# Reordering the four score rounds of an attention segment: keys in the first round, value products in the other three

## The reference

```
x = x + attention0(layernorm(x), ctx)      # 16 heads of 64, softmax over 1024 context rows
x = x + experts0(layernorm(x))             # 32 experts, 6 of them per token, and 2 shared chunks
x = x + attention1(layernorm(x), ctx)
x = x + experts1(layernorm(x))             # 8 experts, one per token, and a shared one

def attention(x, c):                       # x: 4 x 512 x 256, c: 4 x 1024 x 192
    q, k, v = x @ Wq, c @ Wk, c @ Wv       # split in 16 heads
    p = softmax(q @ k.T / 8)
    return (p @ v) @ Wo + bo
```

## Time and profile before

| what | value |
|---|---|
| median of 3 runs | 2790.21 us |
| profiled execution, its own time | 2784.74 us |
| profiled execution, its span | 2783.1 us |
| mean granted TensorE clock | 0.967 |
| TensorE matmul busy | 2576.6 us (93%) |
| VectorE busy | 2074.2 us (75%) |
| GpSimd busy | 1513.9 us (54%) |
| ScalarE busy | 1283.3 us (46%) |

### The profile page before, as it was taken

The page is one execution under the profiler, slowest core; times in us unless marked ns, Lnnn a source line. Parts: engine busy times, 40 slices in busy tenths (PEclk is TensorE's granted clock), DMA queues, the critical chain, the costliest instruction groups (busy, mean ns, idle before and its releaser), DMA issues. The chain is left out here.

```text
span 2783.1 us, 37259 instructions
## 1 busy us (share of the span) xinstructions
PE 2576.6 (93%) x13254; PEld 1779.0 (64%) x13254; DVE 2074.2 (75%) x2464; ACT 1283.3 (46%) x1776; POOL 1513.9 (54%) x1132
## 2 busy tenths in 40 slices
PE   4999999999999689999999689999999999996895
PEld 3656565656565378888888555656565656554784
DVE  5677777777877577777777667777777777765795
ACT  3545454545554333333333345545454545443384
POOL 2777777777786511111111158777777777671345
PEclk8999999999999799999999789999999999997998
DMA  3211221221211100000000021112112121104212
GB/s 108 55 52 43 61 52 52 57 56 42 67 42 48 48 31 27 23 23 23 23 28 17 17 77 49 51 54 55 52 54 59 42 55 42 48 21 161 83 50 88
DMA packets 60160, 141.65 MB, mean 51 GB/s; under 512 B 8448, under 2 KB 21632, under 8 KB 59008
## 3 DMA queue, kind: packets, MB, share of 16 engines
q1 hardware_dynamic: 55184, 132.73, 16.6%
q0 software_dynamic: 1536, 4.20, 0.5%
q10 hardware_dynamic: 3312, 3.02, 0.3%
HBM read 79.36 MB, written 10.22 MB: 32 GB/s over the span
## 5 line engine op out<-in xcount | busy, mean ns | idle before, releaser
L382 POOL TENSOR_TENSOR L0a_psums<-L0a_psums,L0a_probs 128x512 f32<-128x512 f32 x384 | 488.1, 1302 | 21.5 <-ACT L0a_probs L439 17.3
L382 POOL TENSOR_TENSOR L1a_psums<-L1a_psums,L1a_probs 128x512 f32<-128x512 f32 x384 | 488.1, 1301 | 21.5 <-ACT L1a_probs L439 17.3
L516 DVE TENSOR_REDUCE L0a_row_max<-psum 128x2 f32<-128x2048 f32 x128 | 293.6, 2294 | 77.1 <-PE psum L653 76.1
L516 DVE TENSOR_REDUCE L1a_row_max<-psum 128x2 f32<-128x2048 f32 x128 | 293.6, 2294 | 76.8 <-PE psum L653 75.8
L876 POOL TENSOR_TENSOR L0e_w_lo<-L0e_raw,L0e_w_hi 128x768 fp32r<-128x768 f32 x34 | 63.8, 1876 | 496.9 <-ACT L0e_w_hi L890 496.9
L439 ACT ACTIVATE L1a_probs<-psum 128x1024 f32<-128x1024 f32 x256 | 253.2, 1026 | 116.7 <-PE psum L677 116.6
L439 ACT ACTIVATE L0a_probs<-psum 128x1024 f32<-128x1024 f32 x256 | 253.2, 1026 | 116.7 <-PE psum L677 116.7
L930 DVE SCALAR_TENSOR_TENSOR xres<-psum,L0e_weights_of,xres 128x256 f32<-128x256 f32 x544 | 225.6, 477 | 22.3 <-PE psum L1103 21.8
L691 PE MATMUL psum<-L0a_probs,L0a_v 128*64 128x512 f32 x1024 | 242.1, 605 | 0.0
L691 PE MATMUL psum<-L1a_probs,L1a_v 128*64 128x512 f32 x1024 | 241.8, 604 | 0.0
L676 PE MATMUL psum<-L0a_q_hh,L0a_k_st 128*128 128x512 f32 x512 | 210.8, 412 | 13.6 <-ACT L0a_probs L439 12.8
(11 more groups left out here) (357 smaller groups left out, 6119.3 us busy)
## 6 DMA issues: line engine op xcount, KB each, us to landing
L0a_k_hs<-L0a_k_st SPq DMA_DIRECT2D x64, 256.0 KB, 3.6
L1a_k_hs<-L1a_k_st SPq DMA_DIRECT2D x64, 256.0 KB, 3.6
L0a_raw<-in_attention SPq DMA_DIRECT2D x35, 384.0 KB, 3.1
L1a_raw<-in_attention SPq DMA_DIRECT2D x35, 384.0 KB, 3.0
L0e_raw<-in_experts SPq DMA_DIRECT2D x34, 384.0 KB, 3.0
L1weights<-in_sorted SPq DMA_DIRECT2D x2, 6144.0 KB, 18.4
L0a_q_hh<-L0a_q_hh SPq DMA_DIRECT2D x64, 128.0 KB, 2.3
L1a_q_hh<-L1a_q_hh SPq DMA_DIRECT2D x64, 128.0 KB, 2.3
```

The costliest lines, as they stand in the source:

```text
L382: nc.gpsimd.tensor_tensor(psums[:, h, :], a, probs[:, h, kv, :], ALU.add).then_inc(sem["acc"], 1)
L516: nc.vector.reduce_max(row_max[:, qt, 0:2 * 32].rearrange("p (h n) -> p h n", h=2)[:, :, 0], psum[:, 0:4 * BANK].rearrange("p (h k) -> p h ...
```

## The change

Two edits, both in the attention phase and so in both layers. VectorE's low part of the first keys goes from behind the third maximum to behind the first. On TensorE the two key projections go from the second round to the first, and value products 0, 1, 2 go from the first round to the second. The rounds three and four keep theirs.

```
@@ segment(i) on VectorE
                             if i + 1 < SEGMENTS:
                                 for qt in range(QT):
                                     maximum(i + 1, qt)
-                                    if qt == 2 and i + 2 < SEGMENTS:
+                                    if qt == 0 and i + 2 < SEGMENTS:
                                         low_keys(i + 2, 0)
@@ segment(i) on TensorE
-                            FILL = ((0, 1, 2), (), (3, 4, 5), (6, 7))
+                            FILL = ((), (0, 1, 2), (3, 4, 5), (6, 7))
                             for qt in range(QT):
                                 if i + 1 < SEGMENTS:
                                     score(i + 1, qt)
                                 for kv in FILL[qt]:
                                     pv(i, kv)
-                                if qt == 1 and i + 2 < SEGMENTS:
+                                if qt == 0 and i + 2 < SEGMENTS:
                                     for half in range(2):
                                         keys(i + 2, half)
                             total(i)
```

## The result

The changed kernel takes 2831.2 us (median of 4 runs, 2829.94 to 2834.12), the kernel before 2789.94 us. The ratio is 1.0149, 95% interval 1.0131 to 1.0167: 41 us slower, where 47 were forecast (2837.0, range 2822 to 2847). Span of the profiled execution: 2828.4 us against 2783.1, so 45.3 us more, at a mean granted clock of 0.969 against 0.967.

The account below looks back on a forecast made before the run. Each round was taken to be bound by TensorE's or VectorE's closed chain. Transposes moving from 13.42 to 14.20 us gave +0.78 us per segment, times 60 46.8 us, added to 2790.2: 2837.0 us, range 2822 to 2847.

Parts of the forecast that it names:

- Low keys behind the first maximum: Round two: VectorE waits 0.52 us for ScalarE before the low keys; third scores come 0.83 us later, at 7.38.
- Keys in round one: Round one: keys wait for the additions, start at 0.88 us; the round goes from 3.39 to 3.30, gaining 0.09.
- Rounds three and four: TensorE holds both, at 3.39 and 3.43 us; transposes start at 14.20 us and not at 13.42.
- The first half: Stretch after the four rounds, 14.18 us: TensorE is busy for 13.81, so none of the loss is given back.
- the rival at 2811: Low keys do not wait for ScalarE (2808 us), or the first half gives back 0.37 us (2815); chance 0.07.
- Sum: Whole segment: +0.78 us, times 60 segments 46.8 us, giving 2837.0 us; chance 0.85.
- The nothing for segment 30: Segment without keys, an empty round one instead of round two: same work, so no change in time.
- The pairing works: Rival: low keys hidden in round one's end, gaining 3.6 to 6 us, 2784 to 2787 us; chance 0.03.
- The point from which it decides: Round two: for the low keys to be hidden they must start at 2.6 us, through by about 4.0.
- The clock falls once per segment: Rival: TensorE's new gap lowers the clock, 1.68 us per segment, 101 us more, 2938 us; chance 0.03.

Follow-up runs that it names:

- e3: Kernel before with TensorE's edit as in the change, whole low keys behind the second maximum: 2803.6 against 2788.7 us, ratio 1.0050.
- e8: Kernel before with TensorE's edit, low keys split: head 0 behind the first maximum, head 1 behind the second; 2800.7 against 2788.7 us, ratio 1.0038.
- e1: Kernel before with TensorE's edit alone, low keys still behind the third maximum: 2803.6 against 2788.7 us, ratio 1.0054.
- e5: Kernel before with TensorE's edit, low keys split: head 0 behind the second maximum, head 1 behind the third; 2789.8 against 2783.0 us, ratio 1.0027.
- e6: Kernel before with TensorE's edit, keys' half 1 before half 0, low keys split behind second and third maximum: 2785.3 against 2783.0 us, ratio 1.0010.
- e2: Kernel before with VectorE's edit alone, low keys behind the first maximum, keys still in round two: one run, 3178.6 against 2788.7 us.
- e7: Kernel before, TensorE unchanged, low keys split: head 0 behind the third maximum, head 1 behind the fourth; 2786.3 against 2783.0 us, ratio 1.0012.
- e9: Kernel before, TensorE unchanged, low keys split: head 0 behind the second maximum, head 1 behind the third; 2783.8 against 2788.7 us, ratio 0.9983.

## Why the prediction was right

- *Low keys behind the first maximum* (third scores at 7.38 us after the first): right. Wait forecast 0.52, measured 0.54 us; third scores at 318.07 - 310.69 = 7.38. That this is the forecast to 0.01 us is partly luck: the keys started 0.07 late, ScalarE's first activation came 1.43 us behind them and not 1.47, its half 0 was 0.01 shorter, and the release of the third scores took 0.06 and not 0.08. e3 and e8 show the cause to be wait and length together, which make the second maximum late.
- *Keys in round one* (start 0.88, round one 3.30 us, a gain of 0.09): wrong by two small terms. The release from the additions to the keys took 0.15 us (311.49 to 311.64) and not the 0.08 that I had from a maximum to the scores, so the keys started at 0.95. And the scores followed 2.48 us later, not 2.42: the two steps behind the ninth matmul, put at 0.23 each, take 0.55 together (313.57 to 314.12). So round one took 3.43 us, a loss of 0.04, and TensorE's own time for a keys' round is 0.67 + 2.48 = 3.15 us, not 3.08: the old round two was as much TensorE's as VectorE's. The late second scores did not matter to the sum, as the second maximum waits for the low keys anyway. The late start of the keys does stand on the chain that sets the third scores (keys, ScalarE, low keys, second maximum), which is why its 0.07 us had to be made up there. I compared round one with the old round one, though; the right comparison is by filling: in e1 the keys' round went from 3.17 to 3.41 and the value products' stayed at 3.39. That 0.24, less 0.02 in the first half, is the 0.22 us of e1.
- *Rounds three and four* (3.39 and 3.43): 3.39 and 3.39. TensorE's own time in round four is that of the other rounds. The low keys in round four had thus cost 0.09 us and not 0.05, and the transposes start at 14.16 and not 14.20.
- *The first half* gives nothing back: 14.18 against 14.19 us. Right, and with it the rival at 2811 falls.
- *Sum*: +0.72 us per segment for +0.78; 43 us for 46.8, 41 by the medians. The nothing for segment 30, and for the first segment, which was counted like the others, did not come true in the profiled execution: -3.3 and +1.5 us. In the medians these can't be seen apart.
- *The pairing works*: falls. The point from which it decides was not reached; the low keys started at 3.61 and would have had to at 2.6. Even in e5 and e6, where they are hidden behind later maxima, there is no gain over the kernel before, since the keys still wait in round one.
- *The clock falls once per segment*: not in the changed kernel, whose gap is 0.50 us and whose clock is 1.00 in all five stretches. The stretch from 925 us on in the earlier trace rows holds one gap of 0.77 us on TensorE, at a clock of 1.00, so the row did bear on a gap of this length. e2 shows that the mechanism exists in these very rounds, after a gap of 3.90 us. The rule of the Trainium skill (TensorE: Matmul & The Clock Gate, section "A second HAM failure mode: psum-queue depth-cycling") is that recurring short idle gaps make the clock swing. The gaps of 0.21 and 0.50 us, in every regular segment of the changed kernel, do not bear it out. e2's clock does swing in every segment, but behind a gap of 3.90 us, which is not a short one.

## What to carry to other kernels

Where one engine alternates between producing for and waiting on another, write both closed chains of a round down with start-to-start distances. Work put into the waiting engine's room delays that engine by what its own wait plus its length exceed the room by, and the round pays only for what of this delay the engine's spare time in the round (0.27 us here) does not make up. Cutting the work in two (e8) was worth about as much as a place where it need not wait (e3), and both together (e5) more. When work moves up past others, look at what frees its destination: here both banks had been free for over 3 us when the keys came at the old place (0.80 and 0.68 us against 4.05), and at the new one two different waits stood right behind each other. Judge a swap by pairing each filling's round before and after, not the round's number.

## What the runs showed of the hardware

A gap of 3.90 us on TensorE was followed, in the regular segments of e2, by a round at a granted clock of 0.54 on the mean (the levels are 2.4 and 1.2 GHz): 6.05 us instead of 3.39. Gaps of 0.50 us, equally regular, left the clock at 1.00. Segment 30 of the kernel after has a round of scores alone with a gap of 2.39 us, as in the earlier trace rows, but its next twelve value products took 2.79 us and not 4.47. All profiles together, two layers each, show more than that: with the keys in round two (before, e2, e7, e9) the round behind this gap was slow in all eight cases, 4.94 to 5.09 us; with the keys in round one it was slow in six of fourteen (e1 and e6 in the second layer, e3 and e8 in both) and 3.39 us in the other eight. So a gap of 2.39 us can bring the clock down or not, even within one execution; why the one order is hit each time is not shown.

The first segment of a layer, behind a gap of 1.21 us before its first scores, differs in the same way. In the kernel after, the ten key matmuls there ran at a mean granted clock of 0.64 with the scores before them, and the round took 4.74 us, in both layers; in e3 the same round took 3.19 at 1.00.

Releases differ by the pair of engines: from a maximum on VectorE to TensorE's next scores 0.06 to 0.08 us, from VectorE's additions to the keys 0.15, from ScalarE's value copies to the keys 0.14.
